# Eight row counts instead of three for TensorE's expert jobs in a mixture-of-experts block

## The reference, cut to what matters

```python
logits = xf @ Wr + br                          # 1024 tokens x 8 experts
thresh = lax.top_k(logits, 2)[0][:, 1:2]
weights = softmax(where(logits >= thresh, logits, -inf))
h = gelu(einsum('td,edh->eth', xf, W1) + b1)   # 512 -> 2048, per expert
expert_out = einsum('eth,ehd->etd', h, W2) + b2  # 2048 -> 512
out = einsum('etd,te->td', expert_out, weights)
```

## Time and profile before

| | us |
|---|---|
| median of 3 runs | 1778.01 (1775.81 to 1779.83) |
| the profiled execution's span | 1779.7 |
| PE busy | 1681.9 (95%) |
| PEld busy | 1413.7 |
| DVE busy | 879.4 |
| ACT busy | 699.1 |
| POOL busy | 314.1 |
| `up` products, 256 columns, 768 of them | 102.6 |
| `up` products, 384 columns, 384 of them | 74.9 |
| `up` products, 512 columns, 384 of them | 92.8 |
| `down` products, 512 columns, 1056 of them | 262.0 |

### The profile page before, as it was taken

The page is one execution under the profiler, slowest core; times in us unless marked ns, Lnnn a source line. Parts: engine busy times, 40 slices in busy tenths (PEclk is TensorE's granted clock), DMA queues, the critical chain, the costliest instruction groups (busy, mean ns, idle before and its releaser), DMA issues.

```text
span 1779.7 us, 27148 instructions
## 1 busy us (share of the span) xinstructions
PE 1681.9 (95%) x10906; PEld 1413.7 (79%) x10906; DVE 879.4 (49%) x1592; ACT 699.1 (39%) x1314; POOL 314.1 (18%) x257
## 2 busy tenths in 40 slices
PE   7999999999999999999999979984999999999996
PEld 6888888888888888888887757763988888888885
DVE  4344443444344443444344566764667457457742
ACT  5333333333333333333334234443555346346521
POOL 4200211011100111011100432555121011011101
PEclk9999999999999999999999989985999999999998
DMA  6601821011101111011011711114656346336611
GB/s 226 215 4 51 139 62 42 19 51 55 51 7 52 55 51 46 15 51 55 4 61 61 251 54 38 57 38 158 232 170 188 120 129 209 126 114 213 197 25 20
DMA packets 54067, 165.11 MB, mean 93 GB/s; under 512 B 10580, under 2 KB 10964, under 8 KB 53376
## 3 DMA queue, kind: packets, MB, share of 16 engines
q1 hardware_dynamic: 38032, 131.88, 21.2%
q0 software_dynamic: 15888, 31.19, 8.1%
HBM read 143.54 MB, written 55.64 MB: 112 GB/s over the span
## 4 chain that ended last, share of the span: by engine, by line
PE 85%; DVE 5%; ACT 4%; issue 3%; DMA 2%; POOL 1%; another core or an unknown queue 0%; SPq 0%; DVEq 0%; ACTq 0%; POOLq 0%
PE psum L403 62%; PE psum L744 13%; PE psum L408 5%; PE psum L523 4%; ACT P L1332 2%; DVE Wh L797 1%; DMA raw<-in_W 1%; DVE xg L1122 1%; PE psum L605 1%; PE psum L677 0%; DMA ya<-residuals 0%; ACT Wh L1171 0%; DMA raw<-in_Wv 0%; ACT xg L1401 0%
## 5 line engine op out<-in xcount | busy, mean ns | idle before, releaser
L403 PE MATMUL psum<-ctx,Wk 128*128 128x512 f32 x1536 | 384.9, 399 | 0.0
L403 PE MATMUL psum<-Wv,ctx 128*128 128x512 f32 x1536 | 368.7, 389 | 0.0
L403 PEld LDWEIGHTS psum<-Wv,ctx 128*128 128x128 f32 x1536 | 288.3, 188 | 59.7
L403 PEld LDWEIGHTS psum<-ctx,Wk 128*128 128x128 f32 x1536 | 279.2, 188 | 55.6
L880 DVE SCALAR_TENSOR_TENSOR kT<-psum,bkc,kT 128x512 fp32r<-128x512 f32 x128 | 96.1, 751 | 387.6 <-ACT kT L1246 387.6
L403 PE MATMUL psum<-xgT,Wh 128*128 128x256 f32 (+2 forms) x1536 | 270.3, 327 | 10.5 <-issue 10.5
L744 PE MATMUL psum<-Wh,hs 128*128 128x512 f32 x1056 | 262.0, 393 | 6.5 <-DVE hs L1135 6.4
L403 PEld LDWEIGHTS psum<-xgT,Wh 128*128 128x128 f32 x1536 | 240.3, 191 | 32.2 <-issue 12.4
L744 PEld LDWEIGHTS psum<-Wh,hs 128*128 128x128 f32 x1056 | 194.7, 189 | 44.7 <-DVE hs L1135 7.9
L1246 ACT ACTIVATE kT<-psum,bkc 128x512 fp32r<-128x512 f32 x128 | 88.3, 690 | 247.7 <-PE psum L403 247.6
L1412 ACT ACTIVATE gl<-psum,b1c 128x512 f32<-128x512 f32 x128 | 88.2, 689 | 245.2 <-PE psum L403 234.7
(11 more groups left out here) (146 smaller groups left out, 1784.3 us busy)
## 6 DMA issues: line engine op xcount, KB each, us to landing
raw<-in_W SPq DMA_DIRECT2D x128, 512.0 KB, 3.6
expert_rows<-in_spare_rows SPq DMA_DIRECT2D x16, 1042.0 KB, 8.1
raw<-in_ctxT SPq DMA_DIRECT2D x32, 512.0 KB, 4.1
xg<-expert_rows POOLq DMA_DIRECT2D x32, 256.0 KB, 4.5
low_parts<-Olo POOLq DMA_DIRECT2D x32, 128.0 KB, 2.4
oT<-low_parts SPq DMA_DIRECT2D x8, 512.0 KB, 5.1
out_x<-x SPq DMA_DIRECT2D x12, 256.0 KB
xs<-in_x SPq DMA_DIRECT2D x4, 512.0 KB, 7.3
```

The source lines that it names most:

```text
L403: mm = pe.matmul(dst, l, r, start=n == 0, stop=n == len(pairs) - 1)
```

## The change

TensorE's program gets eight unrolled versions of each job, for 128, 224, 256, 288, 336, 384, 448 and 512 rows. `go_on` becomes a chain of seven comparisons. `down` runs over the chunks that hold the width, rounded up. A job of 128 rows has one chunk, so its last product cannot signal both `y_ready` and `y_psum`; TensorE's queue waits for `y_psum` there and then raises `y_ready` by an instruction of its own. GpSimd's three cases, ScalarE and VectorE stay as they are. With the counts above the versions that run are

| job | 0 | 1 | 2 | 3 | 4 | 5 | 6 | 7 |
|---|---|---|---|---|---|---|---|---|
| rows | 264 | 212 | 468 | 166 | 389 | 134 | 83 | 332 |
| width before | 384 | 256 | 512 | 256 | 512 | 256 | 256 | 384 |
| width after | 288 | 224 | 512 | 224 | 448 | 224 | 128 | 336 |
| chunks before | 3 | 2 | 4 | 2 | 4 | 2 | 2 | 3 |
| chunks after | 3 | 2 | 4 | 2 | 4 | 2 | 1 | 3 |

```diff
         NARROW, MIDDLE, WIDE = 256, 384, 512
+        WIDTHS = (128, 224, 256, 288, 336, 384, 448, 512)
...
                 if i == 0:
-                    pe.wait_ge(xgT_lo, CH * q + width // P)
+                    pe.wait_ge(xgT_lo, CH * q + -(-width // P))
...
-                for c in range(width // P):
+                for c in range(-(-width // P)):
                     for m, (x, y) in enumerate(((0, 0), (0, 1), (1, 0))):
                         mm = pe.matmul(bank[3 + c], hr[x][:, c * P:(c + 1) * P], Wh[i][y][:, 512:1024],
                                        start=i == 0 and m == 0, stop=i == NI - 1 and m == 2)
-                    if i == NI - 1 and c == 0:
+                    if i == NI - 1 and c == 0 and width > P:
                         mm.then_inc(y_ready, 1)
                 mm.then_inc(y_psum, 1)
+                if i == NI - 1 and width <= P:
+                    pe.wait_ge(y_psum, n + 1)
+                    pe.sem_inc(y_ready, 1)
...
-                    pe.br_cond(rows_of[q] <= NARROW, f"job{q}_{NARROW}", f"over_narrow_{place}")
-                    with nc.body(f"over_narrow_{place}", valid_engines=only):
-                        pe.br_cond(rows_of[q] <= MIDDLE, f"job{q}_{MIDDLE}", f"over_middle_{place}")
-                    with nc.body(f"over_middle_{place}", valid_engines=only):
+                    over = [f"over_{width}_{place}" for width in WIDTHS]
+                    pe.br_cond(rows_of[q] <= WIDTHS[0], f"job{q}_{WIDTHS[0]}", over[0])
+                    for n, width in enumerate(WIDTHS[1:-1]):
+                        with nc.body(over[n], valid_engines=only):
+                            pe.br_cond(rows_of[q] <= width, f"job{q}_{width}", over[n + 1])
+                    with nc.body(over[len(WIDTHS) - 2], valid_engines=only):
                         pe.br(f"job{q}_{WIDE}")
...
-                for width in (NARROW, MIDDLE, WIDE):
+                for width in WIDTHS:
                     with nc.body(f"job{q}_{width}", valid_engines=only):
                         job(q, width, q + 1 < E)
                         go_on(q + 1, f"{q}_{width}")
```

## The result

The changed kernel takes 1766.58 us (median of 6 runs, 1764.24 to 1772.54) where the kernel before took 1777.99 beside it: ratio 0.994, interval 0.9924 to 0.9956. It is faster by 11.4 us. The forecast was 22 us less, 1756, so the time lies inside the stated range and the gain is half of what was forecast. The execution that was profiled (1772.54 us, span 1770.7) is the longest of the six.

The account below looks back on a forecast made before the run. PE, busy for 95% of the span, was taken as the bound, with VectorE setting job 6. Terms -5.0 - 5.2 - 3.4 - 4.2 - 7.0 + 1.5 + 1.2 = -22.1 us off 1778.0 gave 1756 us, range 1748 to 1768.

Parts of the forecast that it names:

- -7.0: Job 6, one chunk and 128 columns: PE's round falls to 2.02 us, VectorE sets the pace; saves 7.0 us.
- +1.5: End of job 6 and start of job 7: 0.2 us exposed plus 1.3 us of clock loss; costs 1.5 us.
- a clock below 1.00 through a narrow job: Sign listed beforehand that the forecast is wrong: granted clock under full during a narrow job; no size given.
- VectorE's 2.25 us: Job 6's round: VectorE's work of 2.20 us plus a handover, taken as 2.25 us, sets the pace.
- `up` above 256 columns: Products at 288, 448 and 336 columns get shorter: jobs 0, 4 and 7 save 5.0, 5.2 and 3.4 us.
- `up` below 256 columns: Jobs 1, 3 and 5 at 224 columns: weight load is the floor, 0.110 us a product; saves 4.2 us for three.
- the line: Rival: 224-column products follow 0.42 ns a column, 0.106 us each; jobs 1, 3, 5 save 2.1 each, 1754 us; chance 0.14.
- the float32 rate: Rival: products under 256 columns run at the slower float32 rate, 0.376 us at 224; kernel 1924 us; chance 0.13.
- The branches: Extra comparisons ahead of jobs 2 and 4, 0.13 us each taken, are exposed; cost 1.2 us.
- The neighbouring block's loss: Jobs 3 and 5 lose the 253 ns branch to a neighbouring block for a far jump; hidden, put at 0.
- The gaps take the gains: Rival: idle and half clock starting jobs 2, 4, 7, job 6 load-bound, 224 columns worth nothing; 1767 us; chance 0.08.

Follow-up runs that it names:

- e7_fill: Changed kernel plus 12 unread products of 512 columns after the last `down` of each job of 256 rows or fewer; 1753.36 us, ratio 0.9944 to the kernel before.
- e3_up256: Changed kernel, but `up` moves 256 columns where the width is 128, `down` still one chunk; 1745.78 us, ratio 0.989 to the kernel before.
- e8_up192: Changed kernel, but `up` moves 192 columns where the width is 128, `down` still one chunk; 1744.53 us, ratio 0.9899 to the kernel before.
- e5_repeat: The changed kernel as it is, run once more; 1752.32 us, ratio 0.9937 to the kernel before.
- e1_no128: Changed kernel without the width of 128, so job 6 runs 224 columns and two chunks; 1748.45 us, ratio 0.9908 to the kernel before.
- e4_no_sub256: Changed kernel without the widths below 256 (256, 288, 336, 384, 448, 512 remain); 1750.07 us, ratio 0.992 to the kernel before.
- e11_fill_job6: Changed kernel, 12 unread 512-column products after job 5 alone, `y_ready` from job 6's last real product, `y_psum` from an extra one; 1765.36 us, ratio 0.9932.
- e2_only128: Kernel before with 128 as the only new width (128, 256, 384, 512), so job 6 alone changes; 1773.94 us, ratio 1.0055 to the kernel before.
- e6_two_chunks: Changed kernel, but the job of 128 rows runs two chunks of `down`, the second padding; 1754.03 us, ratio 0.9936 to the kernel before.
- e9_signal: Changed kernel, `up` of 192 columns for width 128, `y_ready` from the last real product, `y_psum` from an extra one, no queue wait; 1760.77 us, ratio 0.9891.

## Why the prediction was half right

**Job 6 (-7.0 and +1.5 on record; +6.15 measured) is the step that failed.** The step let PE's round fall to "12 x 0.110 + 3 x 0.232 = 2.02" and VectorE set the pace. It took the full clock for granted, though "a clock below 1.00 through a narrow job" stood among its own signs of being wrong. The record had priced half clock as 1.3 us of loss at a job's start, in the way of job 6 before, where 256 columns follow; what it did not ask is whether the narrow products would win the clock back once it had fallen. They did not, for 37 us of uninterrupted work. The first 36 products take 7.41 us (1630.75 to 1638.16) where 0.107 each would be 3.9, and the seven rounds from 1639.54 to 1667.98 take 1.8 us more each: 3.5 + 12.6 = 16 us lost on PE, more than twice the 7 that the narrower job would have brought. With the clock kept (e7_fill) or soon back (e3_up256, e8_up192) the job takes 44.8 to 45.1 us, which is 7.2 to 7.5 less than before, where 7.0 less 1.5 for the end was on record: about the right size, for a clock that the kernel didn't have.

That it came so near is in part luck. In e8_up192 the stretch from `down(0)` to the end of `up(15)` takes 29.6 us (1618.81 to 1648.40), 3.6 less than the 33.2 on record. The end takes more: from `up(15)` to job 7 it is 9.4 us there and 8.3 in the changed kernel, where 6.9 was on record, because the last `down` waits longer for VectorE (it starts 3.1 us after `up(15)` in the changed kernel) and 4.26 us idle follow it.

What the step is worth in time: e5_repeat (the changed kernel) and e8_up192, run side by side, differ by 7.8 us in their medians. They differ by 14 in job 6 of their profiles, but there one is the longest of its runs and the other the shortest. With the 7.8 back, the gain is 19.7 us of the 22.1 forecast; the rest fits jobs 0 and 4 below, which miss 4.8 us in the profile, less the 2 us that job 6 then has to the good.

**Who sets job 6's round at full clock.** VectorE's 2.25 us was said to. In e8_up192 rounds without turned rows have the length of PE's work, 2.04 us (1625.70 to 1627.74), and PE waits for `hs` only before the last two `down` (1.26 and 1.22 us). `down` runs two rounds behind `up`; so VectorE, which by the earlier trace rows needs 2.20 us a round, can fall behind a little in each and is late only at the end. The step had no such slack, which fits a middle on record that was too long and an end that was too short.

**`up` above 256 columns: right in price.** Measured pitches are 0.132 at 288 (1251.30 to 1252.88 for 12), 0.203 at 448 and 0.153 at 336; on record stood 0.134, 0.200 and 0.154. One `up` of each width on the timeline of PE in the changed kernel:

```profile
1251.30 1.74 PE L404 MATMUL psum<-xgT,Wh 128*128 128x288 f32 x12
1252.88 2.25 PE L745 MATMUL psum<-Wh,hs 128*128 128x512 f32 x9
...
1315.87 1.49 PE L404 MATMUL psum<-xgT,Wh 128*128 128x224 f32 x12
1317.20 1.56 PE L745 MATMUL psum<-Wh,hs 128*128 128x512 f32 x6
...
1506.54 2.60 PE L404 MATMUL psum<-xgT,Wh 128*128 128x448 f32 x12
1508.97 2.90 PE L745 MATMUL psum<-Wh,hs 128*128 128x512 f32 x12
...
1698.37 2.01 PE L404 MATMUL psum<-xgT,Wh 128*128 128x336 f32 x12
1700.21 2.00 PE L745 MATMUL psum<-Wh,hs 128*128 128x512 f32 x8
```

Job 7 gained 3.1 us (3.4 on record, with half clock at its start priced apart, in the +1.5). Job 0 gained 3.0 (5.0): PE now reaches the late weights earlier and waits 2.62 us for them at 1259.33 instead of 0.40. That alone gives nothing back that was forecast, but the wait ends 22.9 us after the job's start, where it was 22.1, and the nine products behind it run at half clock, 3.77 us instead of 2.31. The timeline of the changed kernel at round 3 of job 0:

```profile
1253.27 1.06 ACT L1177 ACTIVATE Wh<-raw 128x1024 fp32r<-128x1024 f32 x1 [3.31 <-DMA raw<-in_W]
...
1259.33 3.77 PE L745 MATMUL psum<-Wh,hs 128*128 128x512 f32 x9 [2.62 <-DVE hs L1141]
```

How long that wait is differs between kernels that do the same there, which is luck as far as the change goes: with the same 288 columns job 0 took 68.4 us in e1_no128, 64.3 in e4_no_sub256 and 63.0 in e7_fill. Job 4 gained 2.4 (5.2): it now starts after 2.69 us idle instead of 1.74, and at half clock (0.83 over its first 8.9 us, has the like for job 6). In the profiles of e4_no_sub256 and e7_fill the clock stays at 1.00 there, and the job gains 4.2 and 3.7 us. The loss of clock at a job's start was on record for job 7 only.

**`up` below 256 columns: right.** 0.111 at 224 (1315.87 to 1317.20), 0.110 at 192 and 0.107 at 128, all at full clock, where 0.110 was on record for 224 and for 128. The weight load is the floor, and both rivals that said otherwise are out: the line (0.106 at 224, 0.066 at 128) and the float32 rate (0.376; the 0.230 that its sum has for 128 columns should be 0.215 at its own 1.68 ns a column, and nothing hangs on it). The Trainium skill's "TensorE: Matmul & The Clock Gate", section "LDWEIGHTS (loading the stationary operand)", gives such a load as its columns over 1.2 GHz, which is 106.7 ns for 128; at full clock the trace agrees to within 5 ns. At half clock the floor is about twice that, 0.205 us a product, which the section does not tell. Jobs 1, 3 and 5 gained 0.7, 1.0 and 1.25 us from start to start (1.4 each on record); that holds the gap behind each, which is wider by 0.56, 0.95 and 0.47.

**The branches: right in size.** A comparison passed lasts 65 ns, and six of them stand some 0.13 us apart ahead of job 2. The branches there, on PE's queue:

```profile
L779 PEldq COMPARE_BRANCH  x6: 65/65/65, 1351.1 to 1351.8; - x6
L781 PEldq COMPARE_BRANCH  x1: 3808/3808/3808, 1351.9 to 1351.9; - x1
```

The gap ahead of job 2 grew from 2.17 to 2.73 us and that ahead of job 4 from 1.74 to 2.69: 1.5 against 1.2. The neighbouring block's loss, put at 0, shows as 0.57 and 0.39 us idle ahead of jobs 3 and 5; there the first `down`'s wait for VectorE got shorter.

**The rivals.** "The gaps take the gains" (0.08, 1767 us) gives the measured time, but by other parts: it held job 6 by its loads at 2.5 us a round, and had the 224 columns worth nothing; of its three starts at half clock those of jobs 4 and 7 came about (job 7's first three `up` take 7.1 us, where 0.153 each would be 5.5), that of job 2 did not. The time was hit by luck, by a sum of parts of which the largest was not in it.

What stays open: what decides, at waits of one to three us, whether the clock falls (e7_fill and e11_fill_job6 differ in it, and the starts of job 2), and what ended the low clock. In all four profiles in which job 6 ran at half clock for over 20 us it rose within about 2 us of the start of a group of turned rows (L409, four products of 128 columns more in the round), which stands at 1667.28 in the changed kernel, 1653.07 in e5_repeat, 1656.00 in e2_only128 and 1653.61 in e11_fill_job6. In the first two an earlier such group did not do it, and no run leaves the turned rows out, so this is an observation and not a cause.

Both profiles of the changed kernel are the longest of their runs (1772.54 of 1764.24 to 1772.54 us, 1759.10 of 1751.71 to 1759.10), so job 6's 58.5 us is above its usual length. An estimate from the mean clocks: 0.001 of it is 3.5 us at half clock in a span of 1757 us, so the other runs of e5_repeat, at 0.967 and 0.968 against 0.964, had 10 to 14 us less at half clock and should be 5 to 7 us shorter; they are 4.6 to 7.4.

## What to carry to other kernels

Price a narrower job at both clocks and ask which one it will run at: the time saved by narrower products was lost twice over here, because the engine entered them slow and did not get back. Below the width at which the weight load is the floor, columns cost next to nothing (0.107 us at 128, 0.110 at 192); padding `up` towards it (192 or 256 here instead of 128) kept the gain of the missing chunk, and the clock came back. Leaving the narrow version out brought nearly as much. And read the clock beside the busy share: PE was at 5.00 of 5.00 us through the slowest stretch of the kernel.

## What the runs showed of the hardware that was not expected

The granted clock stayed at 1.2 GHz through 37 us in which PE never paused, with 12 products of 128 and 3 of 512 columns a round (0.50 in the windows from 1640 to 1665), for as long in e5_repeat and for 30 us in e2_only128. With 6 of 512 it came back after about 11 us (e6_two_chunks, at 1633), and with 192 or 256 columns in `up` after 4 to 7 us (a mean of 0.88 to 0.93 over the job, the gap behind it included). Once at 2.4 GHz, the same 128-column rounds kept it, from 1668 to the next idle time and through all of e7_fill's job. The Trainium skill's "TensorE: Matmul & The Clock Gate", section "What's actually happening", says that the clock follows how busy the engine is and that activity releases it; in the first profile PE shows as busy for 5.00 of 5.00 us at 0.50 and at 1.00 alike, so the busy share that a profile shows does not tell which level is granted.

A jump of TensorE's queue to a far block took 3.4 to 4.5 us in the changed kernel and up to 5.4 us in e7_fill, and in e7_fill and e11_fill_job6 PE idled once more for 1.2 us on "issue", 29 and 19 products behind the jump. The same jump into job 2 took 3.3 us in e9_signal, 3.8 in the changed kernel and 5.1 in e7_fill.
